# Windowed attention: q weights at a step of 4 columns, v windows of 48 rows with both parts side by side

## The reference

```python
x = x + 0.5 * ffn(layernorm(x))        # ffn: x and W rounded to FP6 blocks of 32 with a scale each, x @ W.T + bias
x = x + attention(layernorm(x))
x = x + 0.5 * ffn(layernorm(x))

def attention(x):                      # HEADS = 16 of 32 channels, K = 13 neighbours, NS = 6
    q, k, v = split(x @ qkv_w.T + qkv_b);  q = q * 32 ** -0.5
    # token i attends to the 13 tokens around it (the first or last 13 at a sequence's ends)
    attn = softmax(einsum("bhld,bhlkd->bhlk", q, k[nbr]) + rpb[:, bidx])
    return einsum("bhlk,bhlkd->bhld", attn, v[nbr]) @ proj_w.T + proj_b
```

## Time and profile before

| | us |
|---|---|
| median of 3 runs | 3381.41 (3375.73 to 3384.6) |
| the profiled execution | 3373.88 |
| its span, first to last instruction | 3372.0 |

### The profile page before, as it was taken

How to read it: one execution, slowest core, us unless ns; L and a number is a source line. 1 busy time by engine, 2 the same in 40 slices (tenths; PEclk the granted TensorE clock), 3 DMA queues, 4 the chain that set the end, 5 groups by cost and what they waited for, 6 DMA issues and landing times. The chain is left out here.

```text
span 3372.0 us, 68516 instructions
## 1 busy us (share of the span) xinstructions
PE 3001.5 (89%) x24864; PEld 1829.5 (54%) x24864; DVE 2306.3 (68%) x3170; ACT 1888.3 (56%) x2323; POOL 1911.1 (57%) x1497
## 2 busy tenths in 40 slices
PE   0399999999999999999978999999999999499999
PEld 0244444444444444444447877777777776244444
DVE  7467666666666766666556666666666665799995
ACT  2355555555555555556545666665666666566662
POOL 3354554554455455445326666666666665788883
PEclk9699999999999999999978999999999999699999
DMA  2123233323323323332247767677767674344442
GB/s 76 63 88 113 88 113 113 107 93 115 119 92 113 113 94 106 113 113 95 93 127 187 191 189 191 189 185 194 188 181 194 187 192 117 115 151 149 149 148 86
DMA packets 339610, 449.44 MB, mean 133 GB/s; under 512 B 23048, under 2 KB 254496, under 8 KB 331168
## 3 DMA queue, kind: packets, MB, share of 16 engines
q1 hardware_dynamic: 339360, 445.57, 43.4%
HBM read 243.85 MB, written 201.38 MB: 132 GB/s over the span
## 5 line engine op out<-in xcount | busy, mean ns | idle before, releaser
L761 DVE TENSOR_TENSOR fq_out_lo<-fq_val,fq_out_hi 128x512 f16<-128x512 f32 x384 | 460.7, 1237 | 289.8 <-ACT fq_out_hi L829 289.8
L946 PE MATMUL fq_acc<-fq_y_hi_t,w_qkv 128*128 128x512 f16 x2048 | 614.6, 379 | 1.6 <-ACT fq_y_hi_t L842 1.6
L1186 ACT ACTIVATE att_ctx<-att_o_ps 32x512 f32<-32x512 f32 x512 | 300.9, 588 | 365.0 <-PE att_o_ps L1295 358.7
L829 ACT CAST fq_out_hi<-fq_val 128x512 f16<-128x512 f32 x384 | 237.3, 618 | 319.1 <-DVE fq_val L758 311.0
L1270 PE MATMUL att_s_ps<-att_k,att_q_bd 128*128 128x44 f16 x6144 | 388.4, 217 | 26.2 <-DMA att_q_bd<-q_parts 16.9
L1270 PEld LDWEIGHTS att_s_ps<-att_k,att_q_bd 128*128 128x128 f16 x6144 | 382.1, 170 | 27.0 <-issue 26.0
L946 PE MATMUL fq_acc<-fq_y_lo_t,w_qkv 128*128 128x512 f16 x1024 | 388.5, 379 | 0.0
L946 PEld LDWEIGHTS fq_acc<-fq_y_hi_t,w_qkv 128*128 128x128 f16 x2048 | 200.1, 98 | 243.6 <-ACT fq_y_hi_t L842 1.8
L946 PE MATMUL fq_acc<-w_qkv,fq_y_hi_t 128*128 128x512 f16 x1024 | 304.9, 380 | 16.7 <-ACT fq_val L824 16.7
L966 PE MATMUL fq_acc<-w_ffn,fq_f_hi_t 128*128 128x512 f16 x1024 | 310.7, 386 | 1.4 <-DVE fq_f_lo_t L806 1.4
L632 PE MATMUL ffn_acc<-w_ffn,ffn_hi_t 128*128 128x512 f16 x1024 | 306.8, 381 | 4.5 <-DVE ffn_x_ring L518 4.4
(11 more groups left out here) (188 smaller groups left out, 6510.2 us busy)
## 6 DMA issues: line engine op xcount, KB each, us to landing
att_v<-v_parts SPq DMA_DIRECT2D x96, 704.0 KB
att_k<-k_parts SPq DMA_DIRECT2D x64, 524.0 KB, 7.1
fq_x<-in_L_attn_x SPq DMA_DIRECT2D x32, 1024.0 KB, 6.8
x_after_ffn<-fq_x SPq DMA_DIRECT2D x32, 1024.0 KB, 4.3
att_q_bd<-q_parts SPq DMA_DIRECT2D x512, 64.0 KB, 3.8
att_x<-x_after_ffn SPq DMA_DIRECT2D x32, 1024.0 KB, 5.9
x_after_attention<-att_x SPq DMA_DIRECT2D x32, 1024.0 KB, 9.2
ffn_x_ring<-x_after_attention SPq DMA_DIRECT2D x32, 1024.0 KB, 6.3
```

Of the source, the lines that this page charges most:

```text
L761: dve.tensor_tensor(out=out[1][:, b], in0=val[:, b % RING], in1=out[0][:, b], op=ALU.subtract).then_inc(s["out_lo"], 1)
L829: act.copy(out[0][:, b], val[:, b % RING]).then_inc(s["out_hi"], 1)
L946: op = pe.matmul(acc[:, b % RING], w, m, start=(kc == 0 and (a, c) == (0, 0)), stop=(kc == KC - 1 and (a, c) == PARTS[-1]))
L1186: return act.activation(ctx_f[rows, u.u % 2].rearrange("p g (c q) -> p g c q", q=CHUNK), o_ps[rows, :, :, h, :], ACT.Copy, scale=1.0 / P_UP)
```

## The change

`q_bd` gets a dimension for the unit ahead of the part, and its last dimension has 4 entries (`CHUNKS`) in place of 8: successive columns of a stationary operand lie 4 elements (8 bytes) apart. The scratch tensor for q is laid out as [128, group, part, 4 x 512], and the ACT operation at L824 reorders its columns by unit, not by half group. `queries` still issues 8 DMAs for a half, now one for each set of rows and unit with both parts in it; its pieces are 256 bytes.

The scratch tensor for v holds high and low part of a row side by side (2 KB a row). `values` loads 48 rows for a window in place of 44, in 2 DMAs: rows with both parts to partitions 0 to 47 (pieces of 2 KB) and rows of the high part alone to partitions 48 to 95 (pieces of 1 KB). The low probabilities go to columns 48 to 91 of `prob`, columns 44 to 47 stay zero. The padding of the scratch tensor grows to 10 rows at the end.

```diff
@@ constants @@
+VROWS = 48
+VTAIL = VROWS - CHUNK - NS
@@ setup, SyncE @@
-                            sp.dma_start(scratch["v"][part, at:at + NS, :], zeros[0:NS, :]).then_inc(padded, 16)
+                        for at, rows in ((0, NS), (NS + TOKENS, VTAIL)):
+                            sp.dma_start(scratch["v"][at:at + rows, part, :], zeros[0:rows, :]).then_inc(padded, 16)
@@ ffn_qkv_phase, SyncE @@
-                            place = scratch["q"][part, :, bass.ds(u.n * KC * GROUP, KC * GROUP)]
+                            place = scratch["q"][:, bass.ds(u.n, 1), part, :].rearrange("p t n -> p (t n)")
...
-                            place = scratch["v"][part, bass.ds(u.n * GROUP + NS, GROUP), :]
+                            place = scratch["v"][bass.ds(u.n * GROUP + NS, GROUP), part, :]
@@ ffn_qkv_phase, ScalarE @@
-                            value = value.rearrange("p (a q c) -> p a q c", a=2, q=CHUNK)
-                            total = total.rearrange("p (a c q) -> p a q c", a=2, q=CHUNK)
+                            value = value.rearrange("p (a q c) -> p a q c", a=SUB, q=CHUNK)
+                            total = total.rearrange("p (a c q) -> p a q c", a=SUB, q=CHUNK)
@@ attention_phase @@
-        q_bd = sb("q_bd", [P, 2, 2, KC, P, QCHUNKS], F16)
+        q_bd = sb("q_bd", [P, 2, QUNITS, 2, KC, P, CHUNKS], F16)
@@ attention_phase, SyncE, queries @@
-                        columns = scratch["q"][:, rows, bass.ds(g.n * KC * GROUP, KC * GROUP)].rearrange(
-                            "a p (g n) -> p a g n", g=KC)[:, :, :, half * QCOLS:(half + 1) * QCOLS]
-                        for part in range(2):
-                            sp.dma_start(q_bd[rows, half, part, :, rows, :].rearrange("p g m c -> p g (m c)"),
-                                         columns[:, part]).then_inc(q_loaded[half], 16)
+                        columns = scratch["q"][rows, bass.ds(g.n, 1), :, :].rearrange(
+                            "p t a (g v n) -> v p (t a g) n", g=KC, n=P)
+                        for unit in range(QUNITS):
+                            sp.dma_start(
+                                q_bd[rows, half, unit, :, :, rows, :].rearrange("p a g m c -> p (a g) (m c)"),
+                                columns[half * QUNITS + unit]).then_inc(q_loaded[half], 16)
@@ attention_phase, SyncE, values @@
-                    for part, at in ((0, 0), (0, WIN), (1, 0)):
-                        rows = scratch["v"][part, bass.ds(g.n * GROUP, GROUP + 2 * NS), :]
-                        windows = bass.AP(rows.tensor, rows.offset, [[C, WIN], [CHUNK * C, GROUP // CHUNK], [1, C]])
-                        sp.dma_start(vals[at:at + WIN, g.u, :, part, :], windows).then_inc(v_loaded[g.u], 16)
+                    rows = scratch["v"][bass.ds(g.n * GROUP, GROUP - CHUNK + VROWS), :, :]
+                    for at, parts in ((0, 2), (VROWS, 1)):
+                        windows = bass.AP(rows.tensor, rows.offset,
+                                          [[2 * C, VROWS], [CHUNK * 2 * C, GROUP // CHUNK], [1, parts * C]])
+                        sp.dma_start(vals[at:at + VROWS, g.u, :, 0:parts, :].rearrange("p w a c -> p w (a c)"),
+                                     windows).then_inc(v_loaded[g.u], 16)
@@ attention_phase, GpSimd @@
-                        pool.tensor_tensor(out=prob[:, u.u % 2, :, WIN:2 * WIN], in0=score[:, u.u % 4],
+                        pool.tensor_tensor(out=prob[:, u.u % 2, :, VROWS:VROWS + WIN], in0=score[:, u.u % 4],
@@ attention_phase, TensorE @@
-                        pe.wait_ge(q_loaded[half], 16 * HG * 2 * (g.n + 1))
+                        pe.wait_ge(q_loaded[half], 16 * HG * QUNITS * (g.n + 1))
...
-                                    q = q_bd[:, half, a, kc, :, place % QUNITS * CHUNKS + c]
+                                    q = q_bd[:, half, place % QUNITS, a, kc, :, c]
...
-                        pe.wait_ge(v_loaded[g.u], 16 * 3 * (g.h + 1))
+                        pe.wait_ge(v_loaded[g.u], 16 * 2 * (g.h + 1))
@@ program @@
-        "q": nc.dram_tensor("q_parts", [2, P, KC * TOKENS], F16).ap(),
+        "q": nc.dram_tensor("q_parts", [P, GROUPS, 2, KC * GROUP], F16).ap(),
-        "v": nc.dram_tensor("v_parts", [2, TOKENS + 2 * NS, C], F16).ap(),
+        "v": nc.dram_tensor("v_parts", [NS + TOKENS + VTAIL, 2, C], F16).ap(),
```

More of the change, by code:

```diff
@@ L1003, in attention_phase @@
     QUNITS = UG // 2
-    QCHUNKS = QUNITS * CHUNKS
-    QCOLS = QUNITS * P
     HALF = ROWS // PAIRS
```

## The result

The changed kernel takes 3428.3 us in the median (3417.9 to 3437.4), beside 3378.6 us of the kernel before: a ratio of 1.0146, with an interval of 1.0102 to 1.0189. Forecast were 3262 us (3200 to 3355). The change is slower by about 50 us, outside the range and with the other sign.

A forecast was written before the change was run, and what follows sets the result against it. The prediction took PE's instruction pace in attention as the bound. Quicker score pairs would save 119 us from 3381.4 us, with the DMA work hidden and other parts costing nothing, giving 3262 us (3200 to 3355).

The forecast's parts named there:

- What bounds the kernel: In attention PE's instruction pace bounds the kernel, 8.16 us a unit, with the DMA engines next in line.
- Part 1: Score matmuls in attention: the step of 4 columns cuts a pair from 60 to 40 ns, gaining 119 us.
- The bound of 56 ns: Slowest pace expected for score pairs in attention, that of pairs with adjacent weights; gain then 24 us.
- rival A: Score pairs stay at 60 ns because something other than the column step sets them: 3381 us, chance 0.07.
- the closer end: Fastest pace expected for score pairs in attention, an estimate halving 60 ns to 30; gain then 179 us.
- Another engine next: In attention PE, at 7.20 us a unit, still exceeds DVE 5.66, POOL 5.53 and ACT 5.24; cost nothing.
- Part 2, q: Loading q in attention: twice the packets at half size, for two groups 6.8 us becomes 12 (9.2 to 13.7).
- Part 2, v: Loading v in attention: 48 rows in 2 KB and 1 KB packets, for two groups 20.8 us becomes 22.7.
- my own sum: DMA engines' mean work for two groups in attention, 49.0 becoming 56.1 us, fits PE's 60.3 us at 93%.
- Rival B: In attention q's smaller pieces make the DMA engines the bound; PE waits on `q_loaded`, 3440 us, chance 0.07; pauses lower clock.
- Parts that cost nothing: Outside attention, q and v stores in `ffn_qkv_phase`, ACT's reordering and the padding add no time, hidden behind PE.

The follow-up runs named there:

- e4: The changed kernel with 44 rows of v in place of 48, still 2 transfers: 3260 us, 0.9626 of the kernel before.
- e5: The changed kernel with 44 rows of v, each transfer cut into rows 0 to 31 and 32 to 43: 3393 us.
- e6: The changed kernel with 45 rows of v in place of 48, 2 transfers: 3404 us, 1.0079 of the kernel before.
- e13: The changed kernel with 50 rows of v in place of 48, 2 transfers: 3343 us, 0.9901 of the kernel before.
- e14: The changed kernel with 52 rows of v in place of 48, 2 transfers: 3318 us, 0.9834 of the kernel before.

## Why the prediction was wrong, step by step

- **What bounds the kernel**: right, with a gap. PE was the bound, but I took the pauses "issue" as a fixed part of the loop. In all 13 of the kernel before a packet of instructions is under way, so they depend on the DMA engines.
- **Part 1**: mechanism right, size low. 33 ns a pair, not 40; 1.31 us a unit, not 0.96. The bound of 56 ns and rival A were wrong, and 30 was the closer end: the loads lie only 20 ns above those of adjacent columns. Of the two sentences of the Trainium skill (SBUF — State Buffer, "Door 1: The DMA port swizzle") the first agrees well enough (118 ns at two columns to a line, 98 for adjacent ones), and the second, 8 bf16 for free, is contradicted by 171 ns.
- **Another engine next**: no other compute engine, right. The supply of instructions was not on my list.
- **Part 2, q**: right. A piece of 256 bytes takes 0.514 x 16 x 3.3 us / 1584 = 17 ns when q is alone (I had 18 to 27, and took about 23, so it is just below my lower end):

```profile
DMA packets 1585, 0.40 MB, mean 121 GB/s; under 512 B 1584, under 2 KB 1584, under 8 KB 1584
...
q1 hardware_dynamic: 1584, 0.38, 51.4%
```

- **Part 2, v**: the step that failed, twice. The size: a packet of 2 KB takes 276 ns, not 186. The 186 was a price on 11 engines, and there it holds (e4, 2181 to 2184: 0.710 x 16 x 3 us / 203 = 168 ns, below); with 48 rows on 16 engines it doesn't. The DMA engines are busy for 0.92 x 8 x 900 / 99.8 = 66 us in two groups, where I had summed 56.1, so that with the right size my own sum (66 against PE's 60.3) would no longer have fitted. And the reasoning: I summed the mean share of 16 engines and found it to fit at 93%, where a mean says nothing about a transfer that has to get through at a given moment. I had read that v left engines free (share 0.77 with no gap) and found the rule that 48 rows take all 16, and then wrote that the sum doesn't need it. It was the one line that decided. That rule of the Trainium skill (DMA: Bandwidth & Descriptors, "Why a DMA increments its semaphore by 16 and not by 1") agrees with every case: 11, 12, 15 and 16 in flight for 44, 24, 45 and 48 rows, 10 and 13 for 50 and 52.

```profile
q1 hardware_dynamic: 203, 0.42, 71.0%
```

- **Rival B**, slower by the DMA engines, had the side right (it gave 3440 us, 3428 were measured), but that is luck in the number: not q's small pieces carry it, and there is no wait on `q_loaded` beyond the start. That the measured share, 0.92, is near the 0.93 of my forecast is chance too, as two groups now take 72 us and not 60. Its addition, that pauses lower the clock, held: 67 us in 900.
- **Parts that cost nothing**: right; from 100 to 1680 us PE is busy for 1428.9 us before and 1430.7 after.

That late instructions are held up by v's packets is shown by the order in time of the packets and by e4, e5, e6, e13 and e14, which change rows or cuts of v alone; by which engine instructions come, and why 48 rows on 16 engines move slower than 52 on 13, is not shown.

## What to carry to other kernels

Before making a transfer "even", ask who lives on the engines that it leaves free. A pause that the profile puts down to issue can be, as here, a wait for instructions that come by DMA, and with a long unrolled loop on PE they come all the time (some 110 packets in 900 us); a transfer that holds 15 or 16 engines delayed them here, and the pause then cost the clock as well. So count engines for each transfer (here by the largest divisor up to 16 of the row count), and try a size with fewer engines beside one with more.

## What the runs showed of the hardware

- One row decides: 44 rows of v (11 engines) 3260 us, 45 rows (15 engines) 3404 us; 52 rows (13 engines) 3318 us.
- Loads of weights with columns 16, 8 and 2 bytes apart take 171, 118 and 98 ns; pairs with few columns follow at 60 and 33 ns.
- Instructions are fetched in packets of 16 KB, which mostly take 0.9 to 1.8 us here (median 1.1 before, 1.35 after); PE goes on 1.6 us after one has landed.
- v at partitions 0 to 47 moved at 124 GB/s on 16 engines, and at 163 GB/s, with 52 rows, on 13; a packet of 2 KB took 276 ns with 48 rows (16 engines) and 168 with 44 (11).
